# Reordering around the second batch's first products and the first hidden tile in an adaLN block on one Trainium2 core

## What is computed

```python
mod = (silu(c) @ wmod)                       # sa, ca, ga, sb, cb, gb per batch
ga, gb = sign(ga) * max(|ga|, 0.25), sign(gb) * max(|gb|, 0.25)
h = layernorm(x) * (1 + ca) + sa
x = x + ga * (h @ (weight * block_mask).T + bias)
h = layernorm(x) * (1 + cb) + sb
h1, h3 = h @ (w1 + 2 * b1 @ a1).T, h @ (w3 + 2 * b3 @ a3).T
x = x + gb * ((silu(h1) * h3) @ (w2 + 2 * b2 @ a2).T)
```

## Time and profile before

| what | value |
|---|---|
| median of 3 runs | 254.79 us (254.53 to 255.49) |
| the profiled execution | 254.8 us |
| its span in the trace | 253.0 us |
| busy TensorE / VectorE / ScalarE / GpSimd | 242.7 / 134.4 / 90.3 / 97.8 us |
| TensorE clock granted, mean | 1.0 of full speed |

### The profile page before, as it was taken

The page is one execution under the profiler, slowest core; times in us unless marked ns, Lnnn a source line. Parts: engine busy times, 40 slices in busy tenths (PEclk is TensorE's granted clock), DMA queues, the critical chain, the costliest instruction groups (busy, mean ns, idle before and its releaser), DMA issues.

```text
span 253.0 us, 3398 instructions
## 1 busy us (share of the span) xinstructions
PE 242.7 (96%) x1202; PEld 192.5 (76%) x1202; DVE 134.4 (53%) x215; ACT 90.3 (36%) x152; POOL 97.8 (39%) x102
## 2 busy tenths in 40 slices
PE   7799989897999999999999999999999999999993
PEld 6557866785888888888888878888888888888772
DVE  3668599799899855555555531641233123312224
ACT  2348582843343464464432312121212121212110
POOL 1329792328213130330310270597356335633300
PEclk9999999999999999999999999999999999999999
DMA  6999990021323322232316530040000000000005
GB/s 184 387 370 410 412 372 18 3 86 41 117 91 103 120 71 86 81 84 84 116 51 99 47 22 0 0 166 0 3 1 0 0 3 0 0 0 0 3 1 167
DMA packets 12530, 24.02 MB, mean 95 GB/s; under 512 B 1241, under 2 KB 2649, under 8 KB 12513
## 3 DMA queue, kind: packets, MB, share of 16 engines
q1 hardware_dynamic: 12352, 23.65, 29.4%
q10 hardware_dynamic: 160, 0.15, 0.3%
HBM read 21.18 MB, written 2.10 MB: 92 GB/s over the span
## 4 chain that ended last, share of the span: by engine, by line
PE 80%; DVE 7%; DMA 4%; issue 3%; ACT 2%; POOL 1%; SPq 1%; DVEq 0%; ACTq 0%; POOLq 0%
PE up_a L1106 24%; PE up_b L1106 23%; PE acc L1120 8%; PE acc L1121 8%; PE acc L1119 8%; DMA wa<-in_weight 4%; PE side L1087 2%; DVE wa L777 1%; POOL ht_lo L396 1%; DVE xt L803 1%; DVE stats L680 1%; PE side L1056 1%; PE side L1091 1%; DVE xt L782 1%; PE acc L1056 1%
## 5 line engine op out<-in xcount | busy, mean ns | idle before, releaser
L899 DVE TENSOR_TENSOR g<-up_b,g 128x512 f32<-128x512 f32 (+1 forms) x22 | 15.2, 690 | 64.7 <-PE up_b L1106 64.7
L1120 PE MATMUL acc<-w_lo,g_hi 128*128 128x512 f32 (+1 forms) x88 | 34.7, 394 | 0.0
L1121 PE MATMUL acc<-w_hi,g_lo 128*128 128x512 f32 (+1 forms) x88 | 34.7, 394 | 0.0
L1119 PE MATMUL acc<-w_hi,g_hi 128*128 128x512 f32 (+1 forms) x88 | 34.6, 394 | 0.0
L651 ACT ACTIVATE g<-up_a 128x512 f32<-128x512 f32 (+1 forms) x22 | 13.2, 598 | 58.9 <-PE up_a L1106 58.9
L791 DVE SCALAR_TENSOR_TENSOR raw<-side,raw 128x512 f32<-128x512 f32 (+2 forms) x33 | 21.5, 677 | 23.5 <-PE side L1087 17.0
L658 ACT ACTIVATE g_hi<-g 128x512 fp32r<-128x512 f32 (+1 forms) x22 | 13.9, 634 | 49.6 <-DVE g L899 49.6
L439 POOL TENSOR_TENSOR w_lo<-work,w_hi 128x512 fp32r<-128x512 f32 (+1 forms) x11 | 14.2, 1286 | 41.5 <-ACT w_hi L577 41.5
L570 ACT ACTIVATE w_hi<-raw 128x512 fp32r<-128x512 f32 (+2 forms) x33 | 20.3, 626 | 21.6 <-DVE raw L791 21.6
L903 DVE TENSOR_TENSOR g_lo<-g,g_hi 128x512 fp32r<-128x512 f32 (+1 forms) x22 | 22.5, 1023 | 8.7 <-ACT g_hi L658 8.4
L1106 PE MATMUL up_a<-ht_hi,w_lo 128*128 128x512 f32 (+1 forms) x88 | 24.2, 396 | 1.5 <-DVE w_lo L797 1.5
(11 more groups left out here) (161 smaller groups left out, 378.3 us busy)
## 6 DMA issues: line engine op xcount, KB each, us to landing
raw<-in_ffn SPq DMA_DIRECT2D x33, 256.0 KB, 2.7
wmod_sb<-in_wmod SPq DMA_DIRECT2D x4, 1024.0 KB, 11.1
xt<-in_x SPq DMA_DIRECT2D x8, 256.0 KB, 8.2
wmod_sb<-in_wmod SPq DMA_DIRECT2D x1, 2048.0 KB, 14.9
out<-xt SPq DMA_DIRECT2D x8, 256.0 KB, 2.5
mask_sb<-in_mask SPq DMA_DIRECT2D x4, 256.0 KB, 10.0
wa<-in_weight SPq DMA_DIRECT2D x4, 256.0 KB, 10.1
lora_raw<-in_lora SPq DMA_DIRECT2D x1, 512.0 KB, 10.4
```

Of the source, the lines that this page charges most:

```text
L899: nc.vector.tensor_tensor(g[0:w], up_b[0:w], g[0:w], ALU.mult).then_inc(g_ready, 1)
L1119: nc.tensor.matmul(acc[t][:], hi, down_hi[j][0:w], start=(j == 0), stop=False)
L1120: nc.tensor.matmul(acc[t][:], hi, down_lo[j][0:w], start=False, stop=False)
L1121: last = nc.tensor.matmul(acc[t][:], lo, down_hi[j][0:w], start=False, stop=(j == HT - 1))
```

## The change

It has four parts, all of them order and waits; no arithmetic is added or removed.

1. The bias of batch 1 and its first products are issued bank by bank, in the order in which the banks come free (1, 0, 2, and then 3), each bias behind the whole value that reads its bank.
2. On VectorE, the centres and the norm of tiles 2 and 3 of the third pass stand ahead of the two instructions of the feed-forward gate.
3. Blocks 0 and 1 of the third pass are turned into up_a and up_b, not up_b and up_a, and only the turn into up_b waits for the gate. The waits of the first `up` products follow the banks.
4. On VectorE, the low parts of pieces 2 and 3 stand ahead of the gating of the last attention tile, piece 4 behind it.

```diff
--- before.py
+++ after.py
@@ -66,6 +66,9 @@
 WHOLE_DVE = (4, 5, 6, 7, 9, 11)
 
 X1_POOL = (4, 5, 6, 7)
+
+TURN_BANKS = (1, 0, 2, 3)
+GATE_COPIES = B
 X2_POOL = (0, 1, 2)
 
 
@@ -275,7 +278,7 @@
         def turn_bank(q):
 
             i, k = divmod(q, KT)
-            return (acc[k], (acc[1], acc[0], acc[2], acc[3])[k], (up_b, up_a, *side)[k])[i]
+            return (acc[k], acc[TURN_BANKS[k]], (up_a, up_b, *side)[k])[i]
 
         def attn_bank(b, t):
             return acc[t] if b else front[t]
@@ -860,9 +863,9 @@
             moment(2 * T + 3)
             centres(2 * T)
             columns(1)
-            gates_of(1)
             centres(2 * T + 2)
             norm(2 * T + 3)
+            gates_of(1)
             merge(0)
             merge(1)
             for n in range(LORA_FIRST, LORA_EARLY):
@@ -881,16 +884,18 @@
             merge(3)
             attn_gate(T + 2)
             merge(4)
+            weight_low(2)
+            weight_low(3)
             attn_gate(T + 3)
+            weight_low(4)
             for s in range(B * HT):
                 w = WIDTH[s % HT]
                 more = s + 1 < HT
-                if s + 1 <= HT:
+                if 0 < s <= HT - 1:
                     weight_low(3 * (s + 1) - 1)
-                if more:
-                    if s:
-                        merge(3 * (s + 1))
-                        merge(3 * (s + 1) + 1)
+                if more and s:
+                    merge(3 * (s + 1))
+                    merge(3 * (s + 1) + 1)
                     weight_low(3 * (s + 1))
                     weight_low(3 * (s + 1) + 1)
 
@@ -947,10 +952,12 @@
                         pe.wait_ge(gates_ready, 1)
                     elif k > 1:
                         pe.wait_ge(gate_row_ready, k - 1)
-                elif i == 2 and k < 2:
+                elif i == 2 and k == 0:
 
                     pe.wait_ge(attn_gated, T)
                     pe.wait_ge(cols_ready, 2)
+                elif i == 2 and k == 1:
+
                     pe.wait_ge(gates_ready, 2)
                 elif i == 2:
 
@@ -1031,16 +1038,17 @@
                 nc.tensor.matmul(mask_bank(k)[:, blocks], const[:, BLOCK_ONES:BLOCK_ONES + P], mask_part[:, blocks],
                                  start=True, stop=True).then_inc(mask_out, 1)
 
-            def attend_bias(b):
+            def attend_bias(b, ts=range(T)):
                 if b:
 
-                    pe.wait_ge(gate_row_ready, B)
-                    pe.wait_ge(*h_done(2 * KT - 1))
-                for t in range(T):
+                    pe.wait_ge(gate_row_ready, GATE_COPIES)
+                for t in ts:
+                    if b:
+                        pe.wait_ge(*h_done(KT + TURN_BANKS.index(t)))
                     rows = slice(t * QUAD, (t + 1) * QUAD)
                     nc.tensor.matmul(attn_bank(b, t)[:], ones[rows], bias_parts[rows], start=True, stop=False)
 
-            def attend(b, k, m):
+            def attend(b, k, m, ts=range(T)):
 
                 if m == 0:
                     pe.wait_ge(high_ready, KT * b + k + 1)
@@ -1162,9 +1170,12 @@
             turn(6)
             turn(7)
             attend_last(0)
-            attend_bias(1)
-            for m in range(3):
-                attend(1, 0, m)
+            attend_bias(1, TURN_BANKS[:3])
+            attend(1, 0, 0, TURN_BANKS[:3])
+            attend_bias(1, TURN_BANKS[3:])
+            attend(1, 0, 0, TURN_BANKS[3:])
+            attend(1, 0, 1)
+            attend(1, 0, 2)
             mod_rows_part(1, range(KT))
             attend(1, 1, 0)
             columns(1)
@@ -1190,13 +1201,13 @@
                     pe.wait_ge(high_ready, CHUNKS + T)
                     pe.wait_ge(low_by_pool, CHUNKS + T - len(LOW_DVE))
 
-                pe.wait_ge(*((silu_ready, s) if s else h_done(2 * KT + 1)))
+                pe.wait_ge(*((silu_ready, s) if s else h_done(2 * KT)))
                 up(s, 0, up_a, h1_out)
                 if more and s != 1:
                     merge(3 * (s + 1))
                     merge(3 * (s + 1) + 1)
 
-                pe.wait_ge(*((g_ready, s) if s else h_done(2 * KT)))
+                pe.wait_ge(*((g_ready, s) if s else h_done(2 * KT + 1)))
                 up(s, 1, up_b, h3_out)
                 if s == 1:
                     pe.wait_ge(parts_ready, len(LORA_CUTS))
```

## The result

| kernel | median us | runs | ratio to before, 95% interval |
|---|---|---|---|
| before | 255.26 (254.53 to 255.59) | 6 | |
| changed | 253.44 (253.31 to 253.71) | 6 | 0.9940 (0.9928 to 0.9952) |

The change makes the kernel 0.6% faster. The forecast was 253.5 us. The difference of the medians is 1.8 us. It is that large because the three further runs of the kernel before, taken beside the changed one, were 255.18 to 255.59, above two of the first three. Between the profiled executions (254.8 and 253.31) it is 1.5, and in the two later groups of runs that hold the changed kernel again it is 1.3 and 1.4.

The account below looks back on a forecast made before the run. TensorE bounds the kernel, holding 80% of the chain, so only its waits can be won. An earlier start (0.82 us) plus the low parts' order (0.50) give 1.32 us: 254.8 becomes 253.5 us, range 253.2 to 254.7.

Parts of the forecast that it names:

- The forecast case: Matmul at 63.21 starts 1.32 us earlier, at about 61.9, and the execution takes 253.5 us; chance 0.46.
- Bounds: Only TensorE's waits, 3.0 us behind loading, can be won; the 190 us behind 63.21 move along unless a wait opens.
- the 0.1 for the one more pass: At the biases of 35.77 on TensorE: splitting the four costs one more pass, taken as 0.1 us.
- The way to the low parts: VectorE's piece at 57.64 starts 0.8 us earlier: VectorE ready at 56.80, TensorE delivering at 56.82.
- Behind it: Merge of 67.96 reached at 66.65; rank-16 pieces end at 66.2 to 66.7, just in time; g_lo maybe held off 0.45 us.
- The spread starves: Rival at the merge of 66.65: VectorE keeps GpSimd's second spread out, TensorE waits 0.4 us, 253.9 or 254.3; chance 0.09.
- The collision at the gate: Rival: GpSimd's spread holds off VectorE's second gate instruction, 0.61 us; the sum is 0.9 us, time 253.9; chance 0.28.
- The addition first: Rival: GpSimd's addition of tile 7 takes the port before low part 4; nothing gained, 254.8, or 255.2; chance 0.08.
- Chances: Over 0.5% (1.27 us) faster 0.38, within 0.5% 0.57, over 0.5% slower 0.05.

Follow-up runs that it names:

- the forced one: Changed kernel with TensorE's first two merges ahead of its gate rows, so GpSimd's spread falls under VectorE's norm and gate: 253.63 us beside 254.73, ratio 0.9958.
- Forced: Changed kernel with VectorE's merge of piece 5 between the last gating and low part 4, so GpSimd's addition starts first: 256.21 us beside 254.73, ratio 1.0043.

## Why the prediction was right, and where it wasn't

The forecast case happened: 253.44 for 253.5, 1.26 us of the change for 1.32. That the two times agree to 0.06 us is partly luck: 0.19 us of the 1.45 by which the matmul moved lie ahead of the change, and the kernel before alone spreads from 254.53 to 255.59. By its steps:

- *Bounds.* Only TensorE's waits count, and the 190 us behind the last of them move along: the matmul moved by 1.45 us and the span by 1.5. No wait opened behind.
- *Part 1*: this step failed in its size. It was to gain 0.6 to 0.8 us on TensorE; it gained 11.49 - 11.31 = 0.18. The bias does start 0.87 us earlier (0.08 behind the start of the last whole value, before 0.95). The term that was wrong is the 0.1 for the one more pass: the split cost 0.69. It did no harm, since the step also said that this time is worth nothing at the end, and the run without part 1 shows that.
- *Part 2*: the first turn at 46.61, with the common 0.19 taken off 0.85 us earlier for 0.8. The first weight piece came 47.12 - 46.53 - 0.19 = 0.40 earlier for 0.5. Alone it gives 0.33% (0.84 us by the ratio).
- *Part 3*: put at nothing, and in the time nothing can be measured. The turn into up_b started at 47.10, 0.49 us behind the end of the gate, where the text had 0.6. Without the exchange the first turn came 0.15 us later; by the text's times (gate at 46.7, turn at 46.85) it would not have waited.
- *The way to the low parts*: piece 3 at 56.65, 0.80 us earlier for 0.8. The view shows no wait ahead of it any more, and it stands 0.60 behind the instruction before, VectorE's own pitch. So VectorE sets it now, which is a further reason why 0.1 or 0.2 us on TensorE ahead of it show nowhere.
- *Part 4*: 61.03 + 0.68 - 56.65 = 5.06 us for 5.02, and the instruction that is held off is the one that the text named.
- *Behind it*: the rank-16 pieces end at 63.68 + 2.15 = 65.83, the merges start at 66.52; 0.69 us of slack were left. g_lo wasn't held off by the 0.45 us feared: it took 0.75 (63.01), beside 0.69 before.
- *The spread starves* didn't happen: the two spreads ran from 62.85 to 64.23, 2.29 us ahead of the merges at 66.52. No run forced it.
- *The collision at the gate* didn't happen, first because TensorE was later than thought (the spread started at 46.77, behind the gate instruction), and it wouldn't have cost 0.4 us, as the forced one (0.12 us) shows. The 0.28 given to it were too many: the row at 28.54, where the same instruction ran through, was the better guide.
- *The addition first* didn't happen: it started at 61.19, behind low part 4's 61.03, and waited. Forced, the hold-off had the size of the text. At full clock it took 254.6 to 255.0 us, for the 254.8 of the text. The text missed that TensorE's clock can also fall behind the longer wait: six of the ten executions were 1.4 us slower than that.
- *Chances*: 0.38 was given to a gain of over 0.5%, and 0.57 to less. The measured 0.6% is on the side that was held less likely, though the forecast case itself lay just on it (1.32 us for a bound of 1.27). So near to the bound the chances say little, and so does the side that came.

## What to carry to other kernels

When two engines hold each other off, the order of an engine's instructions has a price of its own: move the instruction that somebody waits for to where the other engine can't have started, and let one that nobody needs soon be held off. Before time is bought on the bounding engine, ask what it waits for next; here 0.2 to 0.5 us gained ahead of a wait were worth nothing, and the two instructions moved on VectorE, which was idle there, gave more than half of the gain. And look at what an instruction's waits really need: a count that covered pieces the next matmuls don't use cost 0.4 to 0.5 us.

## What was not expected of the hardware

- One matmul of 32 rows between matmuls of 128 rows took 0.43 us until the next could start, as long as four that ran side by side (0.44). Splitting four of them and the four products behind into two groups each cost TensorE 0.69 us.
- After a wait of 2.37 us TensorE's granted clock fell to 0.50 for about 3 us in the profiled execution, which cost 1.55 us up to the next merges; six of ten executions show a lowered mean clock and are 1.4 us slower. Behind the waits of 1.49 us (before) and 1.07 us (the change) the traces show 1.00.
- A GpSimd instruction of one operand and 128 elements (0.61 us) hardly holds VectorE off (0.15 us over three instructions), while one of two operands and 512 elements (1.3 us) does. A subtraction of VectorE with both operands in SBUF that starts inside one ends 0.54 to 0.55 us behind it, in all 12 cases of the change's trace.
